# Attention with a maxima pass: three long maxima go from steps 0 to 2 to steps 5 to 8, and the totals' bank joins their ring one step earlier

## What is computed

```python
q = rms_norm(linear(layernorm(x), q_w, q_b), norm_q_w)      # 4 batches, 512 queries, 16 heads of 32
k = rms_norm(linear(ctx[:, 257:], k_w, k_b), norm_k_w)      # 1344 text keys
v = linear(ctx[:, 257:], v_w, v_b)
k_img = rms_norm(linear(ctx[:, :257], k_img_w, k_img_b), norm_k_img_w)   # 257 image keys
v_img = linear(ctx[:, :257], v_img_w, v_img_b)
out = softmax(q @ k.T / sqrt(32)) @ v + softmax(q @ k_img.T / sqrt(32)) @ v_img   # per head
x = x + tanh(g_xattn) * linear(out, o_w, o_b)
x = x + tanh(g_ffn) * ffn(layernorm(x))                     # shared and routed experts
```

## Time and profile before

| | |
|---|---|
| median of 3 runs | 1707.87 us (1707.13 to 1708.17) |
| the profiled execution | 1711.98 us, of which its span is 1710.4 us |
| attention, steps of groups 0 to 15 | the first score at about 396 us, the last exponential at about 1152 us of the span |
| a group in the steady part (from one transposition of maxima to the next) | 45.4 to 45.7 us |
| groups 5 and 9, with the projection of four tiles | 58.0 us |
| granted TensorE clock, mean of the span | 0.994 |

### The profile page before, as it was taken

One profiled execution on the slowest core, in us unless ns is written; L12 is line 12 of the kernel. 1 busy time (PEld: TensorE's weight loads), 2 busy tenths in 40 slices (PEclk: granted clock), 3 DMA queues, 4 the chain that ended last, 5 costly groups with the idle time before them and its releaser, 6 DMA issues. The chain is left out here.

```text
span 1710.4 us, 24784 instructions
## 1 busy us (share of the span) xinstructions
PE 1668.2 (98%) x8694; PEld 1119.6 (65%) x8694; DVE 1184.7 (69%) x2220; ACT 831.6 (49%) x1550; POOL 900.4 (53%) x343
## 2 busy tenths in 40 slices
PE   6999999999999999999999999998999999999999
PEld 5888878886445555455554455445777778888777
DVE  6776677667888887888878888777444454443565
ACT  4443333326666664666556666662221355554221
POOL 3221311215777775788747777710605476775642
PEclk9999999999999999999999999999999999999999
DMA  9556858646556553565455555211314487886533
GB/s 332 167 158 195 242 173 210 195 151 195 154 153 159 147 149 66 154 159 159 137 139 145 157 136 141 101 39 42 136 38 155 163 267 258 271 270 198 174 103 99
DMA packets 198603, 277.34 MB, mean 162 GB/s; under 512 B 30968, under 2 KB 128008, under 8 KB 197964
## 3 DMA queue, kind: packets, MB, share of 16 engines
q1 hardware_dynamic: 192928, 258.91, 51.4%
q0 software_dynamic: 5120, 16.78, 2.9%
q10 hardware_dynamic: 432, 0.07, 0.0%
HBM read 202.21 MB, written 106.42 MB: 180 GB/s over the span
## 5 line engine op out<-in xcount | busy, mean ns | idle before, releaser
L1306 ACT ACTIVATE P<-ps 128x512 f32<-128x512 f32 (+1 forms) x832 | 444.8, 598 | 232.8 <-PE ps L1147 160.3
L1437 DVE TENSOR_REDUCE mp<-ps 128x1 f32<-128x448 f32 x720 | 411.8, 615 | 80.3 <-PE ps L1127 78.2
L1587 POOL TENSOR_TENSOR sacc<-sacc,P 128x2048 f32<-128x2048 f32 x90 | 397.7, 4419 | 16.4 <-ACT P L1306 5.5
L1127 PE MATMUL ps<-Kst,Qst 96*128 96x448 f32 x960 | 336.1, 371 | 2.7 <-DVE stl L626 1.7
L1147 PE MATMUL ps<-Qst,Kst 100*128 100x512 f32 (+1 forms) x832 | 323.5, 411 | 4.0 <-ACT P L1306 3.2
L1127 PEld LDWEIGHTS ps<-Kst,Qst 96*128 96x128 f32 x960 | 182.9, 191 | 156.7 <-DVE mp L1437 86.5
L1081 PE MATMUL ps<-P,Vg 128*32 128x512 f32 (+2 forms) x1664 | 217.5, 607 | 0.4 <-ACT P L1306 0.3
L822 POOL TENSOR_TENSOR cl<-craw,ch 128x1024 fp32r<-128x1024 f32 (+2 forms) x26 | 62.0, 2383 | 283.2 <-ACT ch L550 283.2
L1147 PEld LDWEIGHTS ps<-Qst,Kst 100*128 100x128 f32 (+1 forms) x832 | 153.1, 186 | 71.4 <-ACT P L1306 40.2
L49 PE MATMUL ps<-W,ch 128*128 128x512 f32 (+1 forms) x408 | 162.5, 398 | 0.0
L51 PE MATMUL ps<-W,cl 128*128 128x512 f32 (+1 forms) x408 | 159.7, 392 | 0.0
(11 more groups left out here) (249 smaller groups left out, 3145.1 us busy)
## 6 DMA issues: line engine op xcount, KB each, us to landing
gur<-in_w_gate_up SPq DMA_DIRECT2D x23, 1024.0 KB, 7.7
Kst<-KHd SPq DMA_DIRECT2D x56, 320.0 KB, 4.9
Vd<-vf SPq DMA_DIRECT2D x50, 256.0 KB, 2.1
craw<-in_ctxT SPq DMA_DIRECT2D x24, 512.0 KB, 4.4
KHd<-sth SPq DMA_DIRECT2D x24, 512.0 KB, 3.5
KLd<-stl SPq DMA_DIRECT2D x24, 512.0 KB, 4.9
dnr<-in_w_down SPq DMA_DIRECT2D x23, 512.0 KB
xg<-Xg SPq DMA_DIRECT2D x23, 512.0 KB, 7.9
```

Of the source, the lines that this page charges most:

```text
L1127: ins = pe.matmul(ps[:, bank, 0:c1 - c0], Qst[G % 3][0:96, j, 128 * qt:128 * qt + 128], Kst[s][0:96, j, c0:c1], start=True, stop=True)
L1306: act.activation(P[slot(G, kt)][:m, j, :], ps[:m, 2 + (e - 1) % 3, :], ACT.Exp, scale=SCALE).then_inc(a_exp, 1)
L1437: dve.reduce_max(out, ps[:, bank:bank + k, 0:cols] if k > 1 else ps[:, bank, 0:cols], AX.X).then_inc(d_ra, 1)
L1587: pool.tensor_tensor(sacc[:, h], sacc[:, h], P[slot(G, kt)][:, h], ALU.add).then_inc(g_sum, 1)
```

## The change

Two numbers of `mixed_order` and two tables are different. `UNITS` places 6, 5, 2 maxima in steps 0, 1, 2 in place of 7, 6, 3; 7, 7, 7, 7 in steps 5 to 8 in place of 6, 6, 6, 6; and 4 in place of 5 in step 10. Steps 3, 4, 9, 11 and 12 keep their number. 13 maxima now stand in steps 0 to 2 in place of 16. `mixed_order` begins with 18 long maxima, no longer 21, so that the first image maximum is still the third of step 4. `FOUR` begins with the first maximum of step 3: bank 7 joins the ring in step 3, and the wait for the copy of the image totals stands there.

```diff
--- before.py
+++ after.py
@@ -939,7 +939,7 @@
     LASTG = NKT * (NG - 1)
 
 
-    UNITS = (7, 6, 3, 5, 6, 6, 6, 6, 6, 6, 5, 2, 0)
+    UNITS = (6, 5, 2, 5, 6, 7, 7, 7, 7, 6, 4, 2, 0)
     PLAN = [[1] * n + [0] * (7 - n) for n in UNITS]
     NEV = 64
 
@@ -947,15 +947,15 @@
         blocks = [(j, qt) for j in range(4) for qt in range(4)]
         long = [(c, *x) for c in (0, 1, 2) for x in blocks]
         image = [(3, *x) for x in blocks]
-        order, long = long[:21], long[21:]
+        order, long = long[:18], long[18:]
         for i in range(16):
-            k = (27 * i + 8) // 16, (27 * i + 35) // 16
+            k = (30 * i + 8) // 16, (30 * i + 38) // 16
             order += long[k[0]:k[1]] if i else long[:k[1]]
             order.append(image[i])
-        return order + long[(27 * 15 + 35) // 16:]
+        return order + long[(30 * 15 + 38) // 16:]
 
     EVENTS = [(x,) for x in mixed_order()]
-    FOUR = range(sum(UNITS[:4]), sum(UNITS[:11]))
+    FOUR = range(sum(UNITS[:3]), sum(UNITS[:11]))
 
     def ring_table():
         used = {0: 64, 1: 63, 6: 62, 7: -1}
```

## The result

The changed kernel takes 1713.7 us (median of 8 runs, 1712.94 to 1715.79) where the kernel before takes 1707.64 (8 runs, 1706.69 to 1712.16): a ratio of 1.0034, with a 95% interval of 1.0023 to 1.0045. Made and timed once more it took 1714.96 us beside 1707.07, a ratio of 1.0048 (1.0034 to 1.0062). The change makes the kernel slower by 0.3 to 0.5%. The forecast was 1713.9 us.

A forecast was written before the change was run, and what follows sets the result against it. TensorE bounds the kernel, with ScalarE setting the pace in steps 0 to 3. -0.37 + 0.62 + 0.39 - 0.08 less 0.17 spare gives +0.39 us per steady group; +4.7 steady, +1.3 others, +6.0 total: 1713.9 us, range 1706.5 to 1719.5.

The forecast's parts named there:

- Part A: Step 0 to the weighing of step 3, paced by ScalarE: ends 0.37 us earlier, 0.24 if only shown idle time goes.
- rival (3): Steps 1 and 2: the 1.05 us of bank waits come back whole, GpSimd then sets the group; 1702.5 us, chance 0.08.
- Step 0's maximum: One maximum less in step 0, among scores that wait for exponentials: image totals start when they did, 0 us.
- Bank 7: In step 3 its first maximum waits for the image totals' copy, ended before TensorE comes: 0 us; fourth bank saves nothing.
- Rival (4): Step 3: the new wait for the image totals' copy stops TensorE, each group loses 0.37 us more; 1719 us, chance 0.04.
- Three late maxima and the runs of seven: Steps 5 to 8: three more long maxima, +0.62 us; bank waits in runs of seven, +0.39 us (0 to +0.71).
- part B: From the weighing of step 3 to the last text weighings: TensorE runs without a pause, so nothing covers added maxima.
- (1): Bank waits in the runs of seven don't appear: 0.0 in a steady group, +0.3 in each other; 1708 us, chance 0.20.
- (2): Waits larger (0.71) and gain smaller (0.24): steady group 0.84 us longer, two others about 1.2; 1720 us, chance 0.18.
- The last run: Group's end, step 11: waits of about 0.08 us for exponentials held up by GpSimd go away, -0.08 us.
- The spare time: At the group's end TensorE had 0.17 us to spare before the text part's copy, on which what follows hangs.
- Groups 5 and 9: Two groups with projections: nothing to spare, runs behind steps 5 and 7 wait 0.35 more each, projection -0.3; sum +0.65 each.

The follow-up runs named there:

- run 3: Kernel before with only bank 7 joining the ring in step 3, counts unchanged: 1707.74 us, ratio 0.9998.
- run 4: Kernel before with step 2's third maximum placed behind that step's third score instead of ahead of it: 1709.86 us, ratio 1.0005.
- run 9: Changed kernel with counts 7, 5, 2 in steps 0 to 2, six in steps 3 to 10, two in step 11: 1715.74 us, ratio 1.0015.
- run 2: Changed kernel with bank 7 joining in step 4 again, so the new counts alone: 1715.01 us, ratio 1.0043.
- run 12: Kernel of run 11 with one maximum back from step 10 to step 5: 1707.75 us, ratio 0.9995.
- run 5: Changed kernel with counts 6, 5, 2 in steps 0 to 2, six in steps 3 to 10, three in step 11: 1718.17 us, ratio 1.0062.
- run 11: Counts of run 9 on the changed kernel with the early split of run 6: 1717.07 us, ratio 1.0020.
- run 6: Kernel before with the split earlier: ScalarE's half behind step 0's exponentials, VectorE's subtraction in the middle of step 1: 1707.29 us, ratio 0.9994.
- run 7: Kernel before with both the early split of run 6 and the later third maximum of run 4: 1701.21 us, ratio 0.9956; again 1701.26 us, 0.9963.

## Why the prediction was right, and where it was off

**Part A (forecast -0.37, measured -0.43 in group 3, -0.33 in the mean of the twelve).** Right, and for the reason given: the score that ends the part waits for ScalarE, so the 1.05 us of bank waits couldn't come back whole. That was rival (3). The rule of the Trainium skill that goes with it (Perfetto Trace Analysis, section Optimization Strategy) says that the repeated gap can mean a lack of buffers. The trace agrees that the loads waited for banks, but taking the waits away gave a third of them back. Whether a fourth bank would have done the same isn't shown: in run 3 it joins behind the four waits, which stand there as before. Run 4 got the same place for the weighing of step 3, 13.96, by the order within step 2 alone. Step 0's maximum was worth 0, as put (run 9).

**Bank 7 (forecast 0).** Right for the steady groups, shown by both halves (runs 2 and 3). Rival (4) fell: the copy of the image totals ends at 542.16 + 0.60 = 542.76, and the first load of step 3's maxima comes at 543.90.

**Three late maxima and the runs of seven (forecast +0.62 and +0.39).** The waits measured 0.33 us in group 3 and 0.36 in the mean, the right size in sum. The +0.62 is the work of three long maxima, which part B shows as 0.82 us for four up to step 10 and one less behind it. Rivals (1) and (2) fell with it. Yet the rule for the waits isn't exact: it gave 0.17, 0.06, 0.09 and 0.07 for the four, whose shown waits are nearly equal, and for run 12's run of seven I had counted 0.17 where none is shown.

**The last run (forecast -0.08, measured +0.13, in the mean +0.11).** This term had the wrong sign. Between the weighings of step 10 and the last text weighings there is a maximum less, -0.21 us, but the stretch shrank from 3.31 to 3.23 us only. Weight loads there in the changed kernel:

```profile
571.41 0.19 PEld L1147 LDWEIGHTS ps<-Qst,Kst 100*128 100x128 f32 x1 [0.21 <-ACT P L1306]
571.52 0.19 PEld L1127 LDWEIGHTS ps<-Kst,Qst 96*128 96x128 f32 x1
571.90 0.19 PEld L1147 LDWEIGHTS ps<-Qst,Kst 100*128 100x128 f32 x1 [0.19 <-ACT P L1306]
```

With less work of its own between them, the scores are back at ScalarE's pace, as in steps 0 to 3. I had let only a wait go, and not asked what the thinner run would wait for. So +0.64 stood at the last text weighings of group 3, and +0.75 in the mean, in place of +0.56.

**The spare time (forecast 0.17).** The copy moved by 43.52 - 43.05 = 0.47, so 0.64 - 0.47 = 0.17 was right (0.21 in the mean). "What follows hangs on that copy" was wrong in the kernel before, where VectorE's additions end 0.05 us later. It did little harm here, the copy's chain being the longer one by 0.23 us after the change. Leaving out VectorE's chain was most of the reason why the forecasts of runs 5 and 9 missed, and part of it in run 11.

**Steady group: +0.39 forecast, +0.49 measured.** In the mean of the twelve the last run was 0.19 us worse than put and part A 0.04 worse, the waits 0.03 better; the spare time was 0.04 larger, and in before VectorE's chain had ended the group 0.05 later. (Group 3 alone grew by 0.42 us, as its part A was long in before.)

**Groups 5 and 9 (forecast +0.65, measured +0.95 and +1.04).** Part A gave 0.28 in group 5 (the weighing of step 3 from the place 14.30 to 14.02), and each of the runs behind the projections of steps 4 and 6 shows three waits. Weight loads of the changed kernel in group 5, up to the projection of step 8:

```profile
648.89 0.52 PEld L1127 LDWEIGHTS ps<-Kst,Qst 96*128 96x128 f32 x2 [0.15 <-DVE mp L1437]
649.76 0.19 PEld L1127 LDWEIGHTS ps<-Kst,Qst 96*128 96x128 f32 x1 [0.23 <-DVE mp L1437]
650.29 0.19 PEld L1127 LDWEIGHTS ps<-Kst,Qst 96*128 96x128 f32 x1 [0.23 <-DVE mp L1437]
...
663.47 0.19 PEld L49 LDWEIGHTS ps<-Woh,aTh 128*128 128x128 f32 x1 [0.34 <-DVE mp L1437]
```

Against the 0.23 of the earlier trace rows that is 0.38 us more in the first run (forecast 0.35). The second, at 659.04 to 660.44, shows 0.63 where before showed none: this is the term that was too small. And the projection still waits 0.34 of its 0.45 us: of the 0.3 that I gave back, 0.11 came against before. Its fourth place is worth the 0.3 all the same, as with the counts alone it waits 0.68 (run 2).

**The total.** By the traces the attention grew by 12 x 0.49 + 2.0 = 7.9 us, and the forecast had 6.0. The medians gave 6.1 us the first time and 7.9 the second. The forecast's 1713.9 is so close to 1713.7 partly by luck: its mechanism was right but for the last run, and its sum was some 1.9 us short, 1.2 of it in the steady groups and 0.7 in the other two.

## What to carry to other kernels

Waits that stand on the bottleneck's own rows are worth only what the next engine in line leaves of them: here 0.33 of 1.05 us (0.43 in group 3), as ScalarE's exponentials were next. Before moving work from one stretch to a later one, list every chain that ends the loop, with its own start and distance to the end; two that lie 0.05 us apart both have to get shorter. A helper's small instruction can hold up the long one that sets the pace: look at what runs on the neighbour's row at the moment when the pacing engine starts. That is why run 4 and run 6 gave nothing alone and 0.4% together: run 4 let GpSimd start earlier, into VectorE's subtraction, and run 6 took the subtraction away.

## What the hardware showed that I had not expected

In these traces VectorE and GpSimd hold each other up where both read SBUF. VectorE's subtraction of two SBUF tiles takes 0.68 us alone. In the changed kernel it starts while GpSimd still adds up the `P` of steps 0 and 1 (L1581, up to about 544.75), and takes 1.67:

```profile
543.62 1.67 DVE L1468 TENSOR_TENSOR aTl<-ot,aTh 128x512 fp32r<-128x512 f32 x1
```
```profile
540.01 4.74 POOL L1581 TENSOR_TENSOR sacc<-P 128x1024 f32<-128x1024 f32 x2 [2.67 <-ACT P L1306]
544.89 9.58 POOL L1587 TENSOR_TENSOR sacc<-sacc,P 128x2048 f32<-128x2048 f32 x2
```

The other way round, in run 4, VectorE started first and GpSimd's two additions took 9.65 us instead of the 9.32 of run 7. The Trainium skill, SBUF — State Buffer, says in the section Who interferes with whom that a VectorE instruction with two SBUF inputs contends with a GpSimd instruction that reads SBUF, and in the section Summary: rules for kernel authors that the one issued second fully blocks until the first finishes. The first case agrees: the subtraction ends at 545.29, about 0.54 us after GpSimd's L1581. The second agrees in direction and roughly in size: the subtraction outlasts the addition's start by 543.76 - 543.30 = 0.46 us, and 0.33 us were lost.

The difference is the same everywhere. The subtraction overlaps the start of GpSimd's first addition by 0.23 us in before, 0.40 in the changed kernel and 0.46 in run 4, and that addition takes 4.67, 4.85 and 4.91 us where it takes 4.59 without overlap: the loss is the overlap less some 0.14 us. The other way round VectorE's instruction ends 0.54 or 0.55 us after GpSimd's, its 0.68 less 0.14, and so does L1443 at the group's end. An instruction that is held seems to get through its first 0.14 us; that is a reading of these rows, and no run was made for it.
